# Post-norm attention and a mixture of experts on one core: the index pass of the router in rounded fp32, and two groups of split weights in another place of VectorE's order

## The reference, cut to what matters

```python
x = layernorm(x + attention(x))                     # 2048 tokens x 512, 16 heads, window 256
def ffn(x):
    probs = softmax(x @ W_router.T)                 # 8 experts
    rw, sel = top_k(probs, 2)                       # weights and experts of each token
    combine = zeros((T, 8)).at[arange(T)[:, None], sel].add(rw)
    sh = (silu(g) * u) @ Ws_down                    # g, u = halves of x @ Ws_gate_up, 1408 wide
    shared_out = sh * sigmoid(x @ W_sgate.T)
    gu = einsum('th,ehi->eti', x, We_gate_up)       # 352 wide for each expert
    eo = einsum('eti,eih->eth', silu(gate) * up, We_down)
    return shared_out + einsum('eth,te->th', eo, combine)
x = layernorm(x + ffn(x))
```

## Time and profile before

| | us |
|---|---|
| median of 3 runs (lowest, highest) | 1053.54 (1053.37, 1054.45) |
| the profiled execution's own time | 1054.75 |
| its span, first to last instruction | 1052.9 |
| TensorE busy in it | 1029.8 |
| VectorE, ScalarE, GpSimd busy | 768.0, 639.8, 441.1 |
| mean granted TensorE clock, as a share of full | 0.994 |

### The profile page before, as it was taken

One profiled execution on the slowest core, in us unless ns is written; L12 is line 12 of the kernel. 1 busy time (PEld: TensorE's weight loads), 2 busy tenths in 40 slices (PEclk: granted clock), 3 DMA queues, 4 the chain that ended last, 5 costly groups with the idle time before them and its releaser, 6 DMA issues.

```text
span 1052.9 us, 19789 instructions
## 1 busy us (share of the span) xinstructions
PE 1029.8 (98%) x7120; PEld 844.1 (80%) x7120; DVE 768.0 (73%) x1154; ACT 639.8 (61%) x1310; POOL 441.1 (42%) x536
## 2 busy tenths in 40 slices
PE   7999999999999999999999999999999999999996
PEld 4677777777777776888888888888888888888884
DVE  6878888888888885693767776676677767667465
ACT  4666666666666764343766666566666666666344
POOL 2688887788888831000122222222222222221173
PEclk9999999999999999999999999999999999999998
DMA  5111111111111035626799999999999999999563
GB/s 194 52 33 33 33 33 38 50 32 33 43 33 33 22 91 194 205 71 200 210 263 259 258 271 254 258 263 251 252 276 267 256 264 263 252 244 256 121 206 144
DMA packets 120981, 171.36 MB, mean 163 GB/s; under 512 B 10114, under 2 KB 63746, under 8 KB 120804
## 3 DMA queue, kind: packets, MB, share of 16 engines
q1 hardware_dynamic: 111856, 149.54, 44.8%
q0 software_dynamic: 8736, 20.45, 11.7%
q10 hardware_dynamic: 292, 0.10, 0.0%
HBM read 151.45 MB, written 23.07 MB: 166 GB/s over the span
## 4 chain that ended last, share of the span: by engine, by line
PE 63%; DVE 2%; ACT 1%; POOL 1%; issue 1%; POOLq 0%; ACTq 0%; DVEq 0%
PE up_ps L1587 4%; PE gate_ps L1587 4%; PE up_ps L1589 4%; PE up_ps L1588 4%; PE gate_ps L1589 4%; PE gate_ps L1588 4%; PE down_ps L1622 4%; PE down_ps L1624 4%; PE down_ps L1623 4%; PE e_up_ps L1663 3%; PE e_up_ps L1664 3%; PE e_up_ps L1665 3%; PE e_up_ps L1674 2%; PE e_up_ps L1672 2%; PE e_up_ps L1673 2%; PE e_gate_ps L1672 2%
## 5 line engine op out<-in xcount | busy, mean ns | idle before, releaser
L1036 POOL DMA_INDIRECT sum_dram<-rows,target_i x39 | 62.1, 1592 | 366.6 <-ACT rows L1147 366.6
L1426 DVE TENSOR_TENSOR e_lo<-e_raw,e_hi 128x1408 fp32r<-128x1408 f32 x78 | 126.6, 1623 | 45.4 <-ACT e_hi L1121 45.4
L1121 ACT CAST e_hi<-e_raw 128x1408 fp32r<-128x1408 f32 x78 | 107.5, 1378 | 52.2 <-PE e_up_ps L1674 52.2
L337 ACT ACTIVATE prob<-score_ps,nbias 128x256 f32<-128x256 f32 (+1 forms) x256 | 118.1, 471 | 6.6 <-DVE nbias L466 6.6
L272 POOL TENSOR_TENSOR probT<-probT,masks 128x256 f32<-128x256 f32 x128 | 92.2, 749 | 60.2 <-DVE probT L496 60.2
L1431 DVE TENSOR_TENSOR ed_lo<-ed_raw,ed_hi 128x1024 fp32r<-128x1024 f32 x39 | 47.8, 1225 | 77.7 <-ACT ed_hi L1129 77.7
L1042 POOL DMA_INDIRECT rows<-x_dram,token_i x39 | 53.5, 1371 | 93.7 <-DVE target_i L1393 67.0
L466 DVE TENSOR_REDUCE nbias<-score_ps 128x2 f32<-128x512 f32 (+1 forms) x128 | 86.3, 674 | 4.4
L344 ACT COPY probT<-probT_ps 128x512 f32<-128x512 f32 x64 | 37.6, 587 | 78.3 <-PE probT_ps L612 78.3
L579 PE MATMUL proj_ps<-wqkv_lo,xT_hi 128*128 128x512 f32 x180 | 78.0, 434 | 1.2 <-ACT squares L358 1.2
L1587 PE MATMUL gate_ps<-x_hi,gu_lo 128*128 128x512 f32 x180 | 72.7, 404 | 0.0
(11 more groups left out here) (272 smaller groups left out, 2984.8 us busy)
## 6 DMA issues: line engine op xcount, KB each, us to landing
e_raw<-in_We_gu SPq DMA_DIRECT2D x78, 704.0 KB, 6.0
ed_raw<-in_We_down SPq DMA_DIRECT2D x39, 512.0 KB, 5.3
raw_ring<-in_Ws_gu SPq DMA_DIRECT2D x58, 256.0 KB, 6.3
wd_raw<-in_Ws_down SPq DMA_DIRECT2D x44, 256.0 KB, 6.4
gu_raw<-in_Ws_gu SPq DMA_DIRECT2D x30, 256.0 KB, 6.1
ed_raw<-in_We_down SPq DMA_DIRECT2D x39, 192.0 KB, 6.6
xT_in<-in_xT SPq DMA_DIRECT2D x16, 256.0 KB, 2.8
x_in<-in_x SPq DMA_DIRECT2D x16, 256.0 KB, 3.1
```

Of the source, the lines that this page charges most:

```text
L337: nc.scalar.activation(prob[:, g % 2, h, seen], score_ps[:, h, seen], ACT.Exp, bias=nbias[:, s % 2, head:head + 1], scale=1.0, accum_out=r ...
L1121: nc.scalar.copy(e_hi[:, half * HK:(half + 1) * HK, :], raw_half(i, half)).then_inc(e_hi_made, 1)
L1426: nc.vector.tensor_tensor(e_lo[:, part, :], raw_half(i, half), e_hi[:, part, :].bitcast(FP32), ALU.subtract).then_inc(e_lo_made, 1)
```

## The change

Three edits.

1. **Index.** The one-hot matrices are written as fp32r. Since a weight isn't exact in it, the weight is split into `weight_hi` and `weight_lo`, and a pair's row matrix has three parts (token, hi, lo) of 40 columns each (WIDTH, 39 tiles and one more) instead of two of 39. The matrices no longer lie in `e_raw`, `ed_raw` and `rows` but in `e_hi`, `e_lo`, `ed_hi` and `ed_lo`: the lanes in two pieces (22 and 10 pairs), the rows in three (16, 12 and 4). `index_tokens` stands behind `gate(9)` on TensorE, no longer ahead of it. `take_index` adds up hi and lo, one instruction and one wait more.
2. **Unit weights' remainders.** In those "up" stages that a turn follows, DVE's `split_gu(n + 2)` moves behind that turn's instructions.
3. **Down weights' remainders.** DVE's `split_wd(0)` and `split_wd(1)` move from group 3 of step NB - 1 to group 0 of step NB.

```diff
-        onehot_lane = e_raw[:, 0:PAIRS * P].rearrange("p (i n) -> p i n", n=P)
+        flat = [t[:, :, :].rearrange("p k n -> p (k n)") for t in (e_hi, e_lo, ed_hi, ed_lo)]
+        lanes_of = [(0, 22, flat[0][:, 0:22 * P].rearrange("p (i n) -> p i n", n=P)), (22, PAIRS, flat[2][:, 0:10 * P].rearrange("p (i n) -> p i n", n=P))]
-        onehot_row = [t[:, 0:NB * 2 * TILES].rearrange("p (b a n) -> p b a n", a=2, n=TILES) for t in (ed_raw, scratch)]
+        rows_of = [(first, last, place.rearrange("p (b a n) -> p b a n", a=3, n=WIDTH)) for first, last, place in (
+            (0, NB, flat[1][:, 0:NB * 3 * WIDTH]), (NB, NB + 12, flat[3][:, 0:12 * 3 * WIDTH]), (NB + 12, PAIRS, flat[1][:, NB * 3 * WIDTH:(NB + 4) * 3 * WIDTH]))]
...
-            def onehot_rows(t):
+            def split_weights():
+
+                link(nc.vector.tensor_copy(weight_hi[:, :, :], top[:, :, 0:TOP_K]))
+                link(nc.vector.tensor_tensor(weight_lo[:, :, :], top[:, :, 0:TOP_K], weight_hi[:, :, :].bitcast(FP32), ALU.subtract))
+
+            def onehot_rows(first, last, row):
+
+                t, b, n = first // NB, slice(first % NB, (last - 1) % NB + 1), last - first
+                both = [P, n, WIDTH]
+                hot = row[:, :, 2, :].bitcast(FP32)
+                link(nc.vector.tensor_tensor(row[:, :, 2, :], row_of[:, first:last].unsqueeze(2).to_broadcast(both), iota[:, 0:WIDTH].unsqueeze(1).to_broadcast(both), ALU.is_equal))
+                link(nc.vector.tensor_tensor(row[:, :, 0, :], hot, token[:, b].unsqueeze(2).to_broadcast(both), ALU.mult))
+                link(nc.vector.tensor_tensor(row[:, :, 1, :], hot, weight_hi[:, b, t:t + 1].bitcast(FP32).to_broadcast(both), ALU.mult))
+                link(nc.vector.tensor_tensor(row[:, :, 2, :], hot, weight_lo[:, b, t:t + 1].to_broadcast(both), ALU.mult))
...
-                nc.vector.tensor_copy(weight_of[:, :], e_up_ps[:, TILES:2 * TILES]).then_inc(routed, 1)
+                nc.vector.tensor_copy(aside[:, :], e_up_ps[:, WIDTH:WIDTH + TILES]).then_inc(index_taken, 1)
+                dve.wait_ge(index_taken, 1)
+                nc.vector.tensor_tensor(weight_of[:, :], aside[:, :], e_up_ps[:, 2 * WIDTH:2 * WIDTH + TILES], ALU.add).then_inc(routed, 1)
...
-                if at == NB - 1 and g == 3:
+                if at == NB and g == 0:
                     split_wd(0)
                     split_wd(1)
-                if at == NB and g == 0:
                     multiply(0)
                     split_hidden(0)
...
+            behind_turn = [ORDER[i][1] + 2 for i in range(len(ORDER) - 1) if ORDER[i][0] == "up" and ORDER[i + 1][0] == "turn" and ORDER[i][1] + 2 < NU]
...
                 if stage == "up":
                     multiply(n)
-                    if n + 2 < NU:
+                    if n + 2 < NU and n + 2 not in behind_turn:
                         split_gu(n + 2)
                     split_hidden(n)
...
+                    if ORDER[at - 1][0] == "up" and ORDER[at - 1][1] + 2 in behind_turn:
+                        split_gu(ORDER[at - 1][1] + 2)
...
-                pe.wait_ge(onehots_made, 1)
+                pe.wait_ge(onehots_made, 2)
...
-                    last = nc.tensor.matmul(e_up_ps[:, 0:2 * TILES], onehot_lane[:, i, :], row, start=(i == 0), stop=(i == PAIRS - 1))
+                    last = nc.tensor.matmul(e_up_ps[:, 0:3 * WIDTH], lane, row, start=(i == 0), stop=(i == PAIRS - 1))
...
+                    gate(n)
                     if n == INDEX_AT:
                         index_tokens()
-                    gate(n)
```

More of the change, by code:

```diff
@@ L757, in ffn_phase @@
     PAIRS = TOP_K * NB
+    WIDTH = TILES + 1
     RAW, HALVES = 3, 3
@@ L822, in ffn_phase @@
         slot, row_of, lane_of = sb("slot", [P, PAIRS]), sb("row_of", [P, PAIRS]), sb("lane_of", [P, PAIRS])
+        weight_hi, weight_lo = sb("weight_hi", [P, NB, TOP_K], FP32R), sb("weight_lo", [P, NB, TOP_K])
         token_i, target_i = (sb(name, [P, TILES], mybir.dt.int32) for name in ("token_i", "target_i"))
@@ L866, in ffn_phase @@
         silu_made, h_made, h_hi_made, h_lo_made = map(sem, ("silu_made", "h_made", "h_hi_made", "h_lo_made"))
-        part_mm, part_taken, r_cleared, logit_mm, r_exp_made, route, before_mm, index_mm, routed = map(sem, ("part_mm", "part_taken", "r_cleared", "logit_mm", "router_exp_made", "route", "before_mm", "index_mm", "routed"))
+        part_mm, part_taken, r_cleared, logit_mm, r_exp_made, route, before_mm, index_mm, index_taken, routed = map(sem, ("part_mm", "part_taken", "r_cleared", "logit_mm", "router_exp_made", "route", "before_mm", "index_mm", "index_taken", "routed"))
         chosen_made, before_taken, onehots_made = map(sem, ("chosen_made", "before_taken", "onehots_made"))
@@ L1380, in onehot_lanes @@
             def onehot_lanes():
-                nc.vector.tensor_tensor(onehot_lane, lane_of[:, :].unsqueeze(2).to_broadcast([P, PAIRS, P]),
-                                        iota.unsqueeze(1).to_broadcast([P, PAIRS, P]), ALU.is_equal).then_inc(onehots_made, 1)
+                for first, last, lanes in lanes_of:
+                    both = [P, last - first, P]
+                    nc.vector.tensor_tensor(lanes, lane_of[:, first:last].unsqueeze(2).to_broadcast(both), iota.unsqueeze(1).to_broadcast(both), ALU.is_equal).then_inc(onehots_made, 1)
@@ L1484, in _ @@
             carried["vector"](dve, beside)
-            for stage, n in ORDER:
+            behind_turn = [ORDER[i][1] + 2 for i in range(len(ORDER) - 1) if ORDER[i][0] == "up" and ORDER[i + 1][0] == "turn" and ORDER[i][1] + 2 < NU]
+            for at, (stage, n) in enumerate(ORDER):
                 if stage == "gate":
@@ L1498, in _ @@
                     if n == PREFIX_AT + 2:
-                        onehot_rows(0)
-                        onehot_rows(1)
+                        split_weights()
+                        for piece in rows_of:
+                            onehot_rows(*piece)
                     if n == PREFIX_AT + 3:
@@ L1576, in index_tokens @@
                 pe.wait_ge(route, 1)
-                pe.wait_ge(onehots_made, 1)
+                pe.wait_ge(onehots_made, 2)
                 for i in range(PAIRS):
-                    row = onehot_row[i // NB][:, i % NB, :, :].rearrange("p a n -> p (a n)")
-                    last = nc.tensor.matmul(e_up_ps[:, 0:2 * TILES], onehot_lane[:, i, :], row, start=(i == 0), stop=(i == PAIRS - 1))
+                    lane, = [lanes[:, i - first, :] for first, last, lanes in lanes_of if first <= i < last]
+                    row, = [row[:, i - first, :, :].rearrange("p a n -> p (a n)") for first, last, row in rows_of if first <= i < last]
+                    last = nc.tensor.matmul(e_up_ps[:, 0:3 * WIDTH], lane, row, start=(i == 0), stop=(i == PAIRS - 1))
                 last.then_inc(index_mm, 1)
```

## The result

| | before | after |
|---|---|---|
| median of the runs of one comparison, us | 1053.45 (6 runs) | 1045.79 (6 runs) |
| lowest, highest | 1051.95, 1054.45 | 1044.47, 1049.05 |
| span of the profiled execution | 1052.9 | 1044.7 |

The ratio is 0.9932, with a 95% interval of 0.9919 to 0.9945: 7.2 us, between 5.8 and 8.5. The spans of the two profiled executions differ by 8.2.

What follows compares the result with a forecast made beforehand. TensorE was taken as the bound, busy 1029.8 of 1052.9 us. Savings of 2.8 (index), 3.9 (unit weights' remainders) and 0.5 (down weights' remainders) sum to 7.2 us: 1053.54 - 7.2 = 1046.3 us, range 1044.7 to 1050.2.

Steps and rivals of the forecast that it cites:

- Index pass: Index matmuls on TensorE: 32 fp32r products paced by weight loads at 0.110 us, 3.5 us instead of 7.06.
- up(8): Start of unit 8's up matmuls, delayed by longer index work on VectorE: 0.25 us lost (0 to 0.6).
- The lanes: One-hot lane matrices on VectorE: done at 476.3, before TensorE reaches the index at 477.2, 0.9 us left.
- down(10): Unit 10's down matmuls, late through the wait for unit 12's weight load: 0.5 us lost (0 to 1.5).
- The index in all: Net of the index edit: 3.5 saved in the pass, less 0.25 and 0.5 lost behind it, 2.8 us.
- Unit weights' remainders: Expert's down matmuls no longer wait for `eT_lo` behind `gu_lo` at 13 places: 3.9 us saved (3.0 to 4.0).
- Down weights' remainders: End of attention: the copy `probT` no longer stands behind two `wd_lo`; 0.5 us saved (0 to 0.8).
- Loads that don't bind: Rival, index pass: fp32r weight loads don't set the pace, pass 2.1 us, time 1044.9; chance 0.12.
- No gain from fp32r at this width: Rival, index pass: a product keeps its old 0.220 us, time 1050.0; chance 0.11.
- loads and streams that don't overlap: Rival, index pass: narrow fp32r loads and streams run one after another, pass 14.8 us, time 1057.2; chance 0.02.
- `gu_lo` where it lands: Rival: moved `gu_lo` brings a new wait, or `h_lo` delays `eT_lo` instead; 3.9 us gone, time 1050.2; chance 0.06.
- The clock: Rival: the granted clock drops behind the new index pass, costing 1.7 us, time 1048.0; chance 0.05.

Runs made afterwards that it cites:

- e5b_probe: Changed kernel with four probe passes of 16 fp32r products each ahead of the index pass, differing in weight and moving columns; 1057.69 us in one execution.
- e10_same: The changed kernel once more, no edit, compared with the kernel before; 1046.5 us, ratio 0.9922.
- e6_mid: Changed kernel with `gu_lo` behind `h_lo` but ahead of the turn's `eT_lo`, instead of behind the turn; 1057.86 us, ratio 1.0031 to the kernel before.
- e7_join: Changed kernel with the router's 9-column pass in two halves, behind gate(3) and up(3); 1044.62 us, ratio 0.9905 to the kernel before.
- e11_join: Repeat of the changed kernel with the router's 9-column pass in two halves, behind gate(3) and up(3); 1044.82 us, ratio 0.9911 to the kernel before.
- e1_index: Kernel before with the index edit alone (fp32r, behind gate(9)); 1050.37 us, ratio 0.9975.
- e2_gu: Kernel before with only the unit weights' remainders moved behind the turn; 1049.37 us, ratio 0.9960.
- e4_ahead: Changed kernel with the index pass back ahead of gate(9); 1050.57 us, ratio 0.9971 to the kernel before.
- e9_mix: Changed kernel with the router's 9-column pass cut in three between the matmuls of gate(3); 1045.98 us, ratio 0.9918 to the kernel before.

## Why the prediction was right

It gave 1046.3 (1044.7 to 1050.2); the runs gave 1045.79, 7.2 us by the ratio against 7.2 by the sum. That the two agree to a tenth is luck: the interval is 5.8 to 8.5, the repetition gives 8.2, and by the starts the sum should have been 8.0 to 8.2, since two of its terms were somewhat small. The mechanisms are what the prediction got right. Point by point:

- **Index pass**, 3.5 us instead of 7.06, since the loads set the pace: 3.51, and e5b_probe shows that the pace goes with the weight columns and not with the 120 others. The step on which the rivals turned was right in mechanism and size.
- **up(8)** late by 0.25: 0.26. The lanes ready with 0.9 to spare: 1.0. VectorE's work on the row matrices and the split weights, forecast at 8.1 us, was 8.08 from start to start.
- **down(10)** late by 0.5: not late at all. In the sum it was a loss of 0.5 us, and it is 0. The timeline of the changed kernel has `h_lo` from 498.32 to 499.00 and the matmul that needs it at 499.76, on time:

```profile
498.32 0.68 DVE L1420 TENSOR_TENSOR h_lo<-hidden,h_hi 128x512 fp32r<-128x512 f32 x1
...
499.76 0.40 PE L1641 MATMUL down_ps<-wd_hi,h_lo 128*128 128x512 f32 x1
```

  The count of `routed` came as worked out (481.31 on a timeline that was 0.6 ahead there; 482.07 forecast). But from it to ACT's cast, which waits for the DMA, took 14.8 us instead of 15.7 (14.6 in e10_same). I had taken that time as fixed, and the slack that it left as negative; it was 0.76. The range of 0 to 1.5 held it.
- **A small loss that I had not named**: the first transposes of `e_h` wait for VectorE 0.35 us, before 0.20 (PE's timeline, 509.62). With 0.06 behind the pass it takes back 0.2. It isn't a fixed price of the change: this wait is 0.20 in e10_same, e6_mid and e7_join, 0.37 in e11_join and 0.79 in e1_index, and no run tells what decides it. The index in all: 3.1 by the starts (3.3 in e10_same), 2.6 by e1_index's ratio, 2.8 forecast.
- **Unit weights' remainders**, 3.9 from 12 x 0.27 and 0.6: 4.2 by e2_gu's ratio, 4.5 by the starts. At the 12 places 0.40 + 0.33 became 0.23 + 0.22, 0.28 each, and the 13th place won 0.61 (0.84 became 0.23): 4.0. So the places that the prediction counted gave what it said. The other 0.5, which takes the whole beyond the term's range of 3.0 to 4.0, lies in steps of under 0.05 each, spread over the stretch, which I can't put down to anything. The 13th place kept 0.1 at its second start, 0.33 before and after:

```profile
979.10 0.49 PE L1682 MATMUL e_up_ps<-ed_hi,eT_lo 128*128 128x512 f32 x1
979.43 0.39 PE L1683 MATMUL e_up_ps<-ed_lo,eT_hi 128*128 128x512 f32 x1
```

- **Down weights' remainders**, 0.5: 0.43, and `wd_lo` fits in with 0.30 left.
- **Rivals.** Loads that don't bind, 2.1 us for the pass: refuted by e5b_probe. No gain from fp32r at this width, and loads and streams that don't overlap: refuted by the 0.110 us a product. `gu_lo` where it lands: no new wait, and e6_mid shows what a place one step earlier would have cost. The clock: 1.00 behind the new pass, but only in the place that it has; e4_ahead, with a wait ahead of the pass, met it.

## What to carry to other kernels

Count an edit in starts on the engine that bounds: over 40% of this gain was twelve delays of 0.28 us that no engine's idle time shows, since the records of two matmuls overlap. Where a matmul is narrow, ask what its weight load costs before counting its columns, and make one pass of many columns from several of few. Work that becomes longer on a helper engine is paid for where the next stage waits for it, so move the consumer behind something else, as the gate here hides the 1.85 us by which the lanes come too late for the old place; and take a DMA's landing time as a range of a microsecond, not as a number.

## What the runs showed of the hardware that I had not expected

- fp32r products with 128 weight columns start 0.107 to 0.11 us apart with 40, 120 or 240 columns, 0.164 with 360; with 64 weight columns and 120 others 0.063. The record of such a load says 190 ns (138 with 64), more than the distance from one product to the next.
- A wait of 1.85 us ahead of a narrow pass was followed by the lower clock within the pass, which cost 3.4 us beyond the wait (e4_ahead). The same pass without a wait ahead kept the full clock in every other profile that has it, in e5b_probe behind the 64 probe products too.
- The fall of the clock near 424 us, with TensorE busy in its records throughout, came in most profiled executions and not in all: not in e1_index, whose pass is the same, nor in the two with the pass in halves. It lasted 3.4 us in five traces and 6.8 in five, e9_mix with its three parts mixed with wide matmuls among these. What decides it stays open.
